# Attention on one core: the late sums move into the step of the early ones, and the work beside the steps moves with them

## The reference

```python
def _L0_attn_b_ref(x, W_attn, W_proj):      # x is already layer-normed
    qkv = x @ W_attn.T                       # 128 -> 6 * 128: four query sets, k, v
    parts = jnp.split(qkv, N_QUERY_SETS + 2, axis=-1)
    k = parts[-2].reshape(Bz, Tz, N_HEAD, hd).transpose(0, 2, 1, 3)    # 16 heads of 8
    v = parts[-1].reshape(Bz, Tz, N_HEAD, hd).transpose(0, 2, 1, 3)
    for g in range(N_QUERY_SETS):
        q = parts[g].reshape(Bz, Tz, N_HEAD, hd).transpose(0, 2, 1, 3)
        att = jnp.einsum('bhqd,bhkd->bhqk', q, k) * scale
        att = jax.nn.softmax(jnp.where(causal, att, -jnp.inf), axis=-1)
        y = jnp.einsum('bhqk,bhkd->bhqd', att, v)
        outs.append(y.transpose(0, 2, 1, 3).reshape(Bz, Tz, C))
    return jnp.concatenate(outs, axis=-1) @ W_proj.T
```

## Time and profile before

| | |
|---|---|
| median of 3 runs | 791.18 us (790.78 to 791.28) |
| the profiled execution | 789.12 us |
| its span (first to last instruction of the profile) | 787.4 us |
| TensorE busy | 736.1 us, 93% of the span |
| VectorE busy | 660.6 us, 84% |
| ScalarE busy | 677.5 us, 86% |
| GpSimd busy | 562.6 us, 71% |
| the 256 exponentials (L1300) | 304.6 us busy, 1240 ns each |
| the weighing matmuls (L1365) | 177.3 us busy |
| the score matmuls (L1293) | 103.4 us busy |

### The profile page before, as it was taken

How to read it: one execution, slowest core, us unless ns; L and a number is a source line. 1 busy time by engine, 2 the same in 40 slices (tenths; PEclk the granted TensorE clock), 3 DMA queues, 4 the chain that set the end, 5 groups by cost and what they waited for, 6 DMA issues and landing times.

```text
span 787.4 us, 21234 instructions
## 1 busy us (share of the span) xinstructions
PE 736.1 (93%) x8090; PEld 404.9 (51%) x8090; DVE 660.6 (84%) x1955; ACT 677.5 (86%) x934; POOL 562.6 (71%) x623
## 2 busy tenths in 40 slices
PE   5798999999999999999999999999888999999996
PEld 3345667777775233333333333333334777677774
DVE  7998999899876867879788888788487889989885
ACT  5918999999999988888898898888987999899984
POOL 2898676655446989999999999989995445445542
PEclk9999999999999999999999999999999999999999
DMA  9210000000044244533543333453400000000000
GB/s 271 64 80 28 2 2 2 2 2 2 2 109 109 73 95 97 101 87 89 108 108 100 96 97 98 92 96 82 99 2 1 10 7 14 15 15 15 15 14 18
DMA packets 37964, 45.74 MB, mean 58 GB/s; under 512 B 6137, under 2 KB 23810, under 8 KB 37858
## 3 DMA queue, kind: packets, MB, share of 16 engines
q1 hardware_dynamic: 37858, 44.33, 23.0%
HBM read 27.53 MB, written 16.78 MB: 56 GB/s over the span
## 4 chain that ended last, share of the span: by engine, by line
PE 61%; DVE 24%; issue 6%; ACT 5%; POOL 4%; DMA 0%; DVEq 0%; ACTq 0%; POOLq 0%
PE psum L1015 15%; PE psum L1365 14%; PE psum L946 14%; PE psum L1432 4%; PE psum L1293 4%; DVE mixed L1034 4%; PE psum L1168 3%; DVE o_tok L1375 2%; DVE vstack L1261 2%; PE psum L1235 2%; ACT hidden_first L960 1%; ACT hidden_parts_first L962 1%; PE psum L695 1%; DVE parts L1193 1%; DVE o_rows L1394 1%
## 5 line engine op out<-in xcount | busy, mean ns | idle before, releaser
L1300 ACT ACTIVATE prob<-psum 128x1280 f32<-128x1280 f32 x256 | 304.6, 1240 | 43.0 <-PE psum L1293 36.3
L1309 POOL TENSOR_SCALAR_AFFINE_SELECT prob<-prob 128x768 f32<-128x768 f32 (+1 forms) x384 | 308.1, 840 | 27.0 <-ACT prob L1300 26.9
L946 PE MATMUL psum<-xt_parts,w_parts 128*128 128x512 f16 x768 | 186.6, 379 | 0.0
L1365 PE MATMUL psum<-prob,vstack 128*32 128x512 f32 (+1 forms) x1536 | 177.3, 533 | 6.4 <-DVE o_tok L1375 4.4
L976 POOL TENSOR_TENSOR hidden_parts_second<-hidden_second,hidden_parts_second 128x512 f16<-128x512 f32 x64 | 77.7, 1213 | 94.8 <-ACT hidden_parts_second L962 94.8
L1034 DVE SCALAR_TENSOR_TENSOR mixed<-psum,comb_y,mixed 128x128 f32<-128x128 f32 x512 | 143.1, 339 | 1.6 <-PE psum L1015 1.5
L976 POOL TENSOR_TENSOR hidden_parts_first<-hidden_first,hidden_parts_first 128x512 f16<-128x512 f32 x64 | 79.2, 1238 | 73.0 <-ACT hidden_parts_first L962 73.0
L1293 PE MATMUL psum<-qstack,kstack 32*64 32x512 f16 (+1 forms) x1536 | 103.4, 362 | 1.9 <-ACT prob L1300 1.8
L1293 PEld LDWEIGHTS psum<-qstack,kstack 32*64 32x64 f16 x1536 | 29.9, 101 | 145.9 <-ACT prob L1300 125.2
L946 PEld LDWEIGHTS psum<-xt_parts,w_parts 128*128 128x128 f16 x768 | 70.9, 98 | 64.9 <-issue 1.4
L960 ACT ACTIVATE hidden_second<-psum,b 128x512 f32<-128x512 f32 x128 | 88.3, 690 | 17.3 <-PE psum L946 12.3
(11 more groups left out here) (150 smaller groups left out, 859.6 us busy)
## 6 DMA issues: line engine op xcount, KB each, us to landing
qstack<-qk_parts SPq DMA_DIRECT2D x128, 128.0 KB, 3.6
qk_parts<-parts SPq DMA_DIRECT2D x64, 192.0 KB, 3.2
kstack<-qk_parts SPq DMA_DIRECT2D x128, 32.0 KB, 3.5
stream<-u_folded SPq DMA_DIRECT2D x4, 512.0 KB, 8.2
kept_x<-stream SPq DMA_DIRECT2D x4, 512.0 KB, 2.7
out<-mixed SPq DMA_DIRECT2D x7, 256.0 KB, 2.3
w_whole<-L_ffn_W SPq DMA_DIRECT2D x1, 1024.0 KB, 9.6
taps<-c_taps SPq DMA_DIRECT2D x1, 640.0 KB, 7.7
```

The lines of the kernel that those rows point to most:

```text
L946: last = e.matmul(bank(u % 4), m.w1[:, w_part, ex, cols], xt_parts[:, s, x_part, :], start=(n == 0), stop=(n == len(PRODUCTS) - 1))
L1300: e.activation(prob[:, n % PROBS, 0:COLS], psum[:, TILE * (n % 2):TILE * (n % 2) + COLS], ACT.Exp, scale=SCALE)\
L1309: return e.affine_select(kept, kept, [[0, n] for n in kept.shape[1:-1]] + [[sign, BLK]], ALU.is_ge, 0.0, base=BLK * half, channel_multipli ...
L1365: last = e.matmul(to[SLOT * lane:SLOT * (lane + 1)], vstack[:, b % 2, kind, c * LANES + lane].rearrange("p h r -> p (h r)"), weights_of(q, ...
```

## The change

- The LATE sum stands in the step of the EARLY sum (`n % 4` = 2), right behind it, and no sum stands in `n % 4` = 3. `vector_turn` stands a step sooner too, with `n % 4` = 2.
- GpSimd masks the LATE weights for the second time in the step of the first masking (3), not in the next step behind the first mask of the next quad.
- The token transposes of batch b+2 and VectorE's two copies of them (`vector_at_x_high`, `vector_at_x_low`) stand in step 2 rather than 0; the copies stand ahead of `vector_turn`.
- `vector_rows` stands in step 3 rather than 5, its three transposes in the other order, and counts `rows_up` twice, once for each half; each half of `tensor_project` waits for its own count.
- `vector_attended` stands in steps 7 and 11 rather than 6 and 10 (9 and 11 in the last batch), so behind the `vector_turn` of steps 6 and 10; `vector_v` in step 15 rather than 14.
- The folded tokens are laid out as (early or late, half, 64), so that EARLY and LATE values are full products of 128 tokens: `tensor_v` has six products on 128 x 128 and six on 128 x 64, where it had three and twelve. The queries and keys are read at the matching places.

```diff
--- before.py
+++ after.py
@@ -62,9 +62,11 @@
            ((ACROSS, 0, 0), (ACROSS, 1, BANK), (LATE, 3, 2 * BANK)),
            ((ACROSS, 2, 0), (ACROSS, 3, BANK), (LATE, 0, 2 * BANK)))
 COLS = 2 * BANK + SETS * BLK
-SUMS_Q = (ACROSS, EARLY, LATE)
+
+SUMS_Q = ((), (ACROSS,), (EARLY, LATE), ())
+KINDS = 3
 STEPS_B = 4 * QUADS
-SUMS_B = len(SUMS_Q) * QUADS
+SUMS_B = KINDS * QUADS
 MASKS_Q = 3
 PROBS = 8
 BOUNDED = 4
@@ -1120,13 +1122,14 @@
             e.wait_ge(v_copied, max(1, b - 1))
 
 
-        for at, h in ((0, 1), (P, 1), (P + BLK, 0)):
-            last = e.transpose(bank(at_bank(b))[:, at:at + P], normed[:, HALVES * b + h, :], eye[:])
-        last.then_inc(at_up, 1)
+        to = bank(at_bank(b))
+        for at in (0, P + BLK):
+            e.transpose(to[:, at:at + P], normed[:, HALVES * b + 1, :], eye[:])
+        e.transpose(to[:, P:3 * P].rearrange("p (l h t) -> p l h t", h=HALVES, t=BLK)[:, :, 0], normed[:, HALVES * b, :],
+                    eye[:]).then_inc(at_up, 1)
 
     def at_source(b):
         return bank(at_bank(b))[:, BLK:BLK + SEQ]
-
 
     def scalar_at_x_high(e, b):
         e.wait_ge(at_up, b + 1)
@@ -1229,9 +1232,9 @@
             e.wait_ge(attn_done, HALVES * (BATCH - 2))
         for kind in (EARLY, LATE, ACROSS):
             for i, (w_part, x_part) in enumerate(PRODUCTS):
-                for half in range(HALVES if kind != ACROSS else 1):
-                    rows = slice(BLK * half, BLK * (half + 1)) if kind != ACROSS else slice(0, P)
-                    token = P * half + BLK * kind if kind != ACROSS else P
+                for late in range(2 if kind == ACROSS else 1):
+                    rows = slice(BLK * late, BLK * (late + 1)) if kind == ACROSS else slice(0, P)
+                    token = P * late + BLK if kind == ACROSS else P * kind
                     last = e.matmul(bank(6)[rows, kind * P:(kind + 1) * P],
                                     at_x[:, s, x_part, token:token + rows.stop - rows.start],
                                     wqkv_parts[:, w_part, SETS + 1, :], start=(i == 0), stop=(i == len(PRODUCTS) - 1))
@@ -1281,21 +1284,21 @@
             e.wait_ge(s_stack[s], STACK * (b // 2 + 1))
         for kind, lane, col in STEPS_Q[t]:
             at = slice(SLOT * lane, SLOT * (lane + 1))
-            queries = qstack[at, s, c].rearrange("p g (h l q) -> p h l g q", h=HALVES, q=BLK)
+            queries = qstack[at, s, c].rearrange("p g (l h q) -> p h l g q", h=HALVES, q=BLK)
             for half in range(HALVES):
                 rows = slice(BLK * half, BLK * (half + 1))
                 if kind == EARLY:
-                    key, moving, place = P * half, queries[:, half], to[rows, col:col + BANK]
+                    key, moving, place = BLK * half, queries[:, half], to[rows, col:col + BANK]
                 elif kind == LATE:
-                    key, moving, place = P * half + BLK, queries[:, half, 1], to[rows, col:col + SETS * BLK]
+                    key, moving, place = P + BLK * half, queries[:, half, 1], to[rows, col:col + SETS * BLK]
                 else:
-                    key, moving, place = P + BLK * half, queries[:, 0], to[rows, col:col + BANK]
+                    key, moving, place = P * half + BLK, queries[:, 0], to[rows, col:col + BANK]
                 last = e.matmul(place, kstack[at, s, c, key:key + BLK], moving, start=True, stop=True)
         last.then_inc(scored, 1)
 
     def scalar_exp(e, n):
         if n >= PROBS:
-            e.wait_ge(weighed, len(SUMS_Q) * ((n - PROBS) // 4 + 1))
+            e.wait_ge(weighed, KINDS * ((n - PROBS) // 4 + 1))
         e.wait_ge(scored, n + 1)
         e.activation(prob[:, n % PROBS, 0:COLS], psum[:, TILE * (n % 2):TILE * (n % 2) + COLS], ACT.Exp, scale=SCALE)\
          .then_inc(exped, 1)
@@ -1331,14 +1334,13 @@
         m = MASKS_Q * q
         if t == 0:
             gpsimd_second_half_mask(e, m)
-            if q:
-                gpsimd_first_half_mask(e, m - 1)
         elif t == 1:
             gpsimd_second_half_mask(e, m + 1)
             gpsimd_first_half_mask(e, m)
             gpsimd_first_half_mask(e, m + 1)
         elif t == 3:
             gpsimd_second_half_mask(e, m + 2)
+            gpsimd_first_half_mask(e, m + 2)
 
     def weights_of(q, kind, lane):
 
@@ -1370,7 +1372,7 @@
     def vector_turn(e, t):
         b, c, _ = step_of(4 * t)
         r = t % 2
-        e.wait_ge(weighed, len(SUMS_Q) * (t + 1))
+        e.wait_ge(weighed, KINDS * (t + 1))
         by_token = bank(7).rearrange("p (l g t) -> p g l t", l=2, t=BLK)
         e.transpose(o_tok[:, r, :].rearrange("p (g l t) -> p g l t", l=2, t=BLK), by_token).then_inc(turned, 1)
         heads = o_tok[:, r, :].rearrange("p (n i r) -> p n i r", i=HALVES, r=2 * HD)
@@ -1387,13 +1389,14 @@
         e.wait_ge(o_normed, QUADS * (b + 1))
         if b:
             e.wait_ge(projected, HALVES * b)
+        e.transpose(o_rows[:, 1].rearrange("p g t -> p (g t)"), o_norm[:, 1].rearrange("p n r -> p (n r)"))\
+         .then_inc(rows_up, 1)
 
         blocks = o_norm[:, 0].rearrange("p (g l n) r -> p g l (n r)", g=SETS, l=2)
         rows = o_rows[:, 0].rearrange("p g (l t) -> p g l t", l=2)
         for late in range(2):
-            e.transpose(rows[:, :, 1 - late], blocks[:, :, late])
-        e.transpose(o_rows[:, 1].rearrange("p g t -> p (g t)"), o_norm[:, 1].rearrange("p n r -> p (n r)"))\
-         .then_inc(rows_up, 1)
+            last = e.transpose(rows[:, :, 1 - late], blocks[:, :, late])
+        last.then_inc(rows_up, 1)
 
     def vector_bounds(e, i, upper):
 
@@ -1414,7 +1417,7 @@
         return bank(6) if b + 1 < BATCH else bank(7)
 
     def tensor_project(e, b, h):
-        e.wait_ge(rows_up, b + 1)
+        e.wait_ge(rows_up, HALVES * b + h + 1)
         if b + 3 < BATCH:
             e.wait_ge(lo_done, 3 * (b + 3) + h + 1)
         elif b + 3 == BATCH and h == 0:
@@ -1832,7 +1835,7 @@
     STARTS = [divmod(n, STEPS_B) for n in range(LAST)]
 
     def tensor_beside(e, b, at):
-        if b + 2 < BATCH and at == 0:
+        if b + 2 < BATCH and at == 2:
             tensor_at_x(e, b + 2)
         if b + 2 < BATCH and at in (4, 8, 12):
             tensor_qk(e, b + 2, at // 4 - 1)
@@ -1854,8 +1857,9 @@
             if n > 2:
                 tensor_scores(e, n)
             tensor_beside(e, *STARTS[n])
-            if n >= 4 and n % 4:
-                tensor_weigh(e, n // 4 - 1, SUMS_Q[n % 4 - 1])
+            if n >= 4:
+                for kind in SUMS_Q[n % 4]:
+                    tensor_weigh(e, n // 4 - 1, kind)
 
     def scalar_attention(e):
         for n in range(LAST):
@@ -1869,19 +1873,16 @@
                 scalar_gap(e, second, 0)
 
     def vector_beside(e, b, at):
-        if b + 2 < BATCH and at == 0:
-            vector_at_x_high(e, b + 2)
-            vector_at_x_low(e, b + 2)
         if b + 2 < BATCH and at in (4, 8, 12):
             vector_qk_high(e, b + 2, at // 4 - 1)
             vector_qk_low(e, b + 2, at // 4 - 1)
-        if b and at == 5:
+        if b and at == 3:
             vector_rows(e, b - 1)
         if b >= BOUNDED and b % BOUNDED == 1 and at in (2, 6):
             vector_bounds(e, b // BOUNDED - 1, at // 4)
-        if b and at in (6 if b + 1 < BATCH else 9, 10):
-            vector_attended(e, b - 1, at // 10)
-        if b + 1 < BATCH and at == 14:
+        if b and at in (7 if b + 1 < BATCH else 9, 11):
+            vector_attended(e, b - 1, at // 11)
+        if b + 1 < BATCH and at == 15:
 
             vector_v(e, b + 1)
 
@@ -1909,9 +1910,13 @@
 
     def vector_attention(e):
         for n in range(LAST):
-            if n % 4 == 3 and n >= 4:
+            b, at = STARTS[n]
+            if at == 2 and b + 2 < BATCH:
+                vector_at_x_high(e, b + 2)
+                vector_at_x_low(e, b + 2)
+            if n % 4 == 2 and n >= 4:
                 vector_turn(e, n // 4 - 1)
-            vector_beside(e, *STARTS[n])
+            vector_beside(e, b, at)
 
     def gpsimd_attention(e):
         for n in range(LAST):
@@ -1923,7 +1928,6 @@
             if n == LAST - STEPS_B + 1:
                 gpsimd_xt_low(e, second, 0)
             gpsimd_mask(e, n)
-        gpsimd_first_half_mask(e, MASKS_Q * QUADS * BATCH - 1)
```

## The result

The changed kernel takes **802.61 us**, the median of 4 runs from 799.32 to 804.45; the kernel before, on the same chip, 791.23 (4 runs, 790.78 to 791.68). The ratio is **1.0139**, 95% interval 1.0105 to 1.0173: slower by 11 us, and above the range of 788 to 801. The profiled execution is the slowest of the four (804.45, span 802.7); before, the span was 787.4. The two profiled executions differ in more than the change: the mean granted clock of this one is 0.988, that of the one before 0.999. By run, the four times of the changed kernel go with it: 799.32 at 0.997, 802.26 and 802.95 at 0.992, 804.45 at 0.988.

The account below looks back on a forecast made before the run. TensorE's order was taken to bound the attention. Common batches (+0.2 each, +2.6), range test +2 and ends +1 - 2 sum to 3.6, called +4: 789.12 becomes 793.1, plus 2.06 gives 795 us; range 788 to 801.

Parts of the forecast that it names:

- The two waits go, -0.74: TensorE's waits before the projection of step 7 (0.24) and the transposes of step 0 (0.50) vanish: -0.74 us a batch.
- EARLY and LATE together, -0.4: LATE right behind EARLY in one step saves TensorE 0.10 us, four times a batch; ends 0 and 0.14 each.
- Rival 3: Merged sums save nothing, since each group's 0.10 belongs to its start: 6 us more, 801 us; chance 0.07.
- Uneven steps, +0.81: Steps 3 and 4 lose 0.39 us, 15 and 0 lose 0.42, against the exponential's floor of 1.83 for two steps.
- A new wait, +0.5: Queries and keys of steps 8 and 12 wait for `vector_attended` behind the turn: 0.25 us, twice a batch.
- The range test, +2: In batches 5, 9 and 13 step 6's test (0.98) stands between turn and sum, delaying TensorE: +2 us in all.
- Twelve products, nothing: Values' products in steps 15 and 0, twelve instead of fifteen: nine slots either way, no change in time.
- GpSimd, nothing: A quad's masks take 5.0 us at most of 5.4, and the second LATE mask comes 0.9 earlier: no change.
- Ends, +1 - 2: Last two batches: transposes in step 0 of batch 15 wait for the values' copy, +1 us; last quad's routing sooner, -2.
- Rival 1: The new wait before queries and keys is hidden and the kernel gets faster: -4.5 us, 786.5 us; chance 0.2.
- rival 4: The parts cancel: with a new wait of 0.1 instead of 0.25 the sum is 0, 791 us; chance 0.18.
- The 2.06 from the profiled execution to the median: The median time was taken to stand 2.06 us above the profiled execution: 793.1 becomes 795 us.

Follow-up runs that it names:

- Experiments 6 and 7: Kernel before with one early part alone: rows in step 3 instead of 5, 793.32 us; token transposes and their copies in step 2 instead of 0, 793.18 us.
- experiment 3: Changed kernel with GpSimd's second masking of each place covering one query set of four only, part of the masking left out: 789.74 us (one run).
- experiment 1: Changed kernel with the upper range test of batches 5, 9 and 13 in step 9 instead of step 6: 798.53 us.
- experiment 4: Changed kernel with eighteen products for the values, all as pairs on halves of the array: 800.96 us (one run).
- experiments 8 and 2: 8: kernel before with LATE behind EARLY in one step, 804.33 us. 2: changed kernel with VectorE's turn a step later and `vector_attended` ahead of it, 791.66 us.

## Why the prediction was wrong

The direction and most of the mechanism were right; 795 was 7.6 us short of 802.61. Point by point:

- *The two waits go, -0.74*: right. Experiments 6 and 7 add that this was no free gain. They went because the early turn moved VectorE's whole queue forward; alone, each came back elsewhere.
- *EARLY and LATE together, -0.4*: right, and better, 0.14 each, -0.56, the upper end. Rival 3 is out.
- *Uneven steps, +0.81*: right, 0.61 + 0.42 - 0.22 = 0.81, at the two places named, with the 1.83 as the floor.
- *A new wait, +0.5*: **the step that failed.** Place and chain were right; 0.25 twice was in truth 1.01 and 0.29 (idle times of 0.93 and 0.22), with ends given as 0 and 0.4. I took the multiply's 0.50 from the earlier trace rows, while the changed turn of step 6 meets a mask that has just started, and its multiply takes 1.15. The price of 0.50 held only where that mask had 0.23 left to run. With the masks lighter the multiply takes 0.42 and the waits are 0.28 and 0.29, near the forecast (experiment 3). The sum also had nothing between the end of VectorE's sum and the start of queries and keys, which is 0.15 (438.45 to 438.60); in step 12 a multiply of 0.43 hid that. Together this is 0.80 a batch, 10 us over 13, more than the whole miss of 7.6; the merging gave 2 us of it back, and the range test took 2 to 4 more. Against the sum of 3.6 the two profiled executions are 15.3 apart.
- *The range test, +2*: short. The test itself took 1.13, the wait it made went from 0.93 to 1.99, and the half clock behind it took another 1.5; moving it away gave 4 to 6 us (experiment 1). That a longer wait could take the clock down was no step of the prediction at all.
- *Twelve products, nothing*: right for the time (experiment 4). The overhead that the Trainium skill gives each matmul (TensorEngine Tiling (Array Packing), Instruction Overhead), an extra 1 us by the prediction's working, can't be seen in the batch, since the exponential's floor covers it. The group gives no sign of a price for each product, with 0.73 for fifteen, 0.73 for twelve and 0.63 for eighteen.
- *GpSimd, nothing*: right, 3.7 us of weight loads behind masks. The reason given, that the second LATE mask no longer queues behind a mask of the next quad, is the one that experiments 8 and 2 speak for (25.5 and 4.9). But GpSimd's masks did decide the case, by way of VectorE's multiply, which the prediction didn't look at.
- *Ends, +1 - 2*: the first steps of batch 15 took 3.2 more, not 1, about 1.5 of it at half clock; the end behind them gained 2.7, not 2. Batches 0 and 1, put at +0.2 together, took 0.9.
- Rival 1 (the wait is hidden) and rival 4 (the parts cancel) both rested on the size of this one wait, and fall with it.
- *The 2.06 from the profiled execution to the median*: it goes with the clock. The profiled one before has a mean of 0.999, runs near the median have 0.994 in the later sets.

What stays open: why a clock drop follows some waits of 1.5 to 2 us and not others, though the four runs' clocks (0.997 to 0.988) say that most of their scatter, 799.32 to 804.45, is the number of such drops. The run with the fewest, 799.32, is still 4 us above the forecast.
